# Attention and W_o products in two parts: the high copies' matmuls ahead of the low copies' wait

## What is computed

```python
scores = jnp.einsum('bhqd,bhkd->bhqk', q, k) * scale
scores = jnp.where(causal[None, None], -jnp.inf, scores)
probs = jax.nn.softmax(scores.astype(jnp.float32), axis=-1).astype(q.dtype)
attn = jnp.einsum('bhqk,bhkd->bhqd', probs, v)
...
attn = attn + io
out = attn.transpose(0, 2, 1, 3).reshape(B, S, NH * VD) @ W_o
```

## Time and profile before

| | us |
|---|---|
| median of 3 runs | 686.48 |
| lowest and highest of them | 684.96, 688.63 |
| the profiled execution's own time | 685.76 |
| its span, first to last instruction | 683.9 |

### The profile page before, as it was taken

How to read it: one execution, slowest core, us unless ns; L and a number is a source line. 1 busy time by engine, 2 the same in 40 slices (tenths; PEclk the granted TensorE clock), 3 DMA queues, 4 the chain that set the end, 5 groups by cost and what they waited for, 6 DMA issues and landing times.

```text
span 683.9 us, 14087 instructions
## 1 busy us (share of the span) xinstructions
PE 645.7 (94%) x4456; PEld 582.5 (85%) x4456; DVE 474.8 (69%) x1291; ACT 400.3 (59%) x934; POOL 371.9 (54%) x331
## 2 busy tenths in 40 slices
PE   8899989999999999999999999999999999889895
PEld 5788987898889988898889888988899888779895
DVE  4877367565766667666856586658666667897996
ACT  4884346744764475646664757456744767445552
POOL 7873368463844473456627472738454715431564
PEclk9999999999999999999999999999999999999998
DMA  7307142410451046103610342114510482000001
GB/s 233 115 2 176 41 93 50 114 56 16 109 132 54 0 99 154 54 0 92 146 46 23 92 101 60 54 46 92 115 54 0 108 240 75 10 1 1 1 17 47
DMA packets 23551, 49.85 MB, mean 73 GB/s; under 512 B 3168, under 2 KB 16352, under 8 KB 21600
## 3 DMA queue, kind: packets, MB, share of 16 engines
q1 hardware_dynamic: 22144, 47.82, 27.3%
q10 hardware_dynamic: 1376, 1.64, 0.7%
HBM read 16.94 MB, written 1.05 MB: 26 GB/s over the span
## 4 chain that ended last, share of the span: by engine, by line
PE 55%; DVE 14%; ACT 13%; issue 11%; POOL 4%; DMA 1%; DVEq 0%; ACTq 0%; POOLq 0%; SPq 0%
PE J L840 9%; PE J L842 9%; PE J L841 9%; PE J L873 4%; ACT Pb L1157 4%; DVE PTl L1298 4%; ACT kvraw L1252 3%; PE SC L860 3%; DVE SC L1367 3%; PE SC L862 3%; PE SC L861 3%; PE SC L864 3%; PE SC L863 3%; POOL rstd L711 3%; ACT PTh L1140 2%
## 5 line engine op out<-in xcount | busy, mean ns | idle before, releaser
L1298 DVE TENSOR_TENSOR PTl<-J,PTh 128x512 fp32r<-128x512 f32 (+1 forms) x192 | 102.8, 553 | 67.4 <-ACT PTh L1140 66.4
L1157 ACT ACTIVATE Pb<-SC,nm 128x128 f32<-128x128 f32 (+7 forms) x128 | 94.9, 741 | 54.8 <-DVE nm L1367 54.3
L1367 DVE CUSTOM_DVE_ANT_0 SC<-SC,mask 128x128 f32<-128x128 f32 (+7 forms) x128 | 97.1, 759 | 21.2 <-PE SC L864 20.0
L873 PE MATMUL J<-ident,Pb 128*128 128x128 f32 x576 | 88.9, 280 | 6.4 <-ACT Pb L1157 5.1
L840 PE MATMUL J<-PTh,Vh 128*128 128x256 f32 x320 | 88.7, 277 | 6.4 <-DVE PTl L1298 6.3
L1140 ACT ACTIVATE PTh<-J 128x512 fp32r<-128x512 f32 (+1 forms) x192 | 88.1, 492 | 8.3 <-PE J L873 7.6
L841 PE MATMUL J<-PTl,Vh 128*128 128x256 f32 x320 | 89.5, 280 | 0.0
L842 PE MATMUL J<-PTh,Vl 128*128 128x256 f32 x320 | 89.5, 280 | 0.0
L873 PEld LDWEIGHTS J<-ident,Pb 128*128 128x128 f32 x576 | 64.3, 141 | 15.4 <-ACT Pb L1157 6.8
L840 PEld LDWEIGHTS J<-PTh,Vh 128*128 128x128 f32 x320 | 60.2, 188 | 13.9 <-DVE PTl L1298 12.8
L860 PE MATMUL SC<-KNh,QNh 128*128 128x128 f32 (+2 forms) x192 | 69.3, 361 | 0.1
(11 more groups left out here) (305 smaller groups left out, 1886.5 us busy)
## 6 DMA issues: line engine op xcount, KB each, us to landing
KK<-RK SPq DMA_DIRECT2D x30, 512.0 KB, 6.3
QS<-RQh SPq DMA_DIRECT2D x15, 256.0 KB, 7.5
QS<-RQl SPq DMA_DIRECT2D x15, 256.0 KB, 6.5
KX<-KX SPq DMA_DIRECT2D x14, 256.0 KB, 2.3
QX<-QX SPq DMA_DIRECT2D x14, 256.0 KB, 2.4
r_kv<-in_W_ckv SPq DMA_DIRECT2D x7, 384.0 KB, 3.5
r_o<-in_W_o SPq DMA_DIRECT2D x18, 128.0 KB, 2.1
r_qn<-in_W_qT SPq DMA_DIRECT2D x16, 128.0 KB, 2.1
```

The source lines that it names most:

```text
L873: last = pe.transpose(o[:, tile(j - 4 * c)], Pb[i % 2][:, tile(j)], ident[:, :])
L1157: act.activation(Pb[i % 2][:, w], SC[i % 2][:, s], ACT.Exp, bias=nm[:, i % 2:i % 2 + 1], scale=-1.0, accum_out=sm[:, b, i:i + 1]).then_inc ...
L1298: dve.tensor_tensor(o, i, h.bitcast(F32), ALU.subtract).then_inc(done[kind], 1)
L1367: dve.tensor_tensor_reduce(out=SC[i % 2][:, s], in0=SC[i % 2][:, s], in1=mask[:, 128 * (7 - i):S], scale=-SCALE, scalar=HIGH, op0=ALU.add, ...
```

## The change

In `pv` the three matmuls of each key block are no longer together. First come, for all blocks, the two that read the high copy PTh (with Vh and with Vl); the step waits for the high copies alone, `hi["tc"]`. Then it waits for `pt_lo`, and then come the matmuls with PTl for all blocks. In `wo` the first wait is for `hi["pv"]`; the wait for `done["pv"]` stands before the third matmul, the first to read ATl. The matmuls are the same in number and size, and their order in the sum changes. The other engines' code is as before.

```diff
--- before.py
+++ after.py
@@ -879,10 +879,14 @@
                         pe.wait_ge(done["vs"], g // 2 + 1)
                 elif g == 0:
                     pe.wait_ge(done["vs"], h + 2)
+                parts = [(j, slice(0, 256) if j <= 2 * g else slice(128, 256)) for j in range(2 * g + 2)]
+                pe.wait_ge(hi["tc"], NCH * h + CH0[2 * g + 2])
+                for j, q in parts:
+                    mm(o[:, q], lhsT=Vh[b][:, j, :], rhs=PTh[:, j, q], start=j == 0, stop=False)
+                    mm(o[:, q], lhsT=Vl[b][:, j, :], rhs=PTh[:, j, q], start=False, stop=False)
                 pe.wait_ge(pt_lo, NCH * h + CH0[2 * g + 2])
-                for j in range(2 * g + 2):
-                    q = slice(0, 256) if j <= 2 * g else slice(128, 256)
-                    last = three(o[:, q], Vh[b][:, j, :], Vl[b][:, j, :], PTh[:, j, q], PTl[:, j, q], j == 0, j == 2 * g + 1)
+                for j, q in parts:
+                    last = mm(o[:, q], lhsT=Vh[b][:, j, :], rhs=PTl[:, j, q], start=False, stop=j == 2 * g + 1)
                 return last
 
             def side(c, o):
@@ -1021,10 +1025,14 @@
                 if kind == "pv":
                     last = pv(u, b, c, o)
                 if kind == "wo":
-                    pe.wait_ge(done["pv"], count("pv", u, c))
+                    pe.wait_ge(hi["pv"], count("pv", u, c))
                     for t in range(2):
-                        last = three(o[:, 256 * t:256 * t + 256], ATh[c % 2][:, tile(t)], ATl[c % 2][:, tile(t)],
-                                     ABh[b][:, 256:512], ABl[b][:, 256:512], True, True)
+                        z, ah, al = slice(256 * t, 256 * t + 256), ATh[c % 2][:, tile(t)], ATl[c % 2][:, tile(t)]
+                        mm(o[:, z], lhsT=ah, rhs=ABh[b][:, 256:512], start=True, stop=False)
+                        mm(o[:, z], lhsT=ah, rhs=ABl[b][:, 256:512], start=False, stop=False)
+                        if t == 0:
+                            pe.wait_ge(done["pv"], count("pv", u, c))
+                        last = mm(o[:, z], lhsT=al, rhs=ABh[b][:, 256:512], start=False, stop=True)
                 if kind == "side":
                     if c == 0:
                         pe.wait_ge(ld_side, LD_SIDE)
```

## The result

| | before | changed |
|---|---|---|
| median of 8 runs, us | 686.73 | 682.61 |
| lowest to highest | 684.96 to 688.63 | 681.20 to 684.23 |
| ratio, 95% interval | | 0.9937 (0.9919 to 0.9954) |
| profiled execution: time, span, clock | 685.76, 683.9, 0.992 | 682.62, 680.8, 0.991 |

The kernel is 4.1 us faster; forecast were 681.6 us and 4.9 us less.

What follows compares the result with a forecast made beforehand. TensorE was busy nearly throughout, but the chain that ended last ran only 55% over it. Terms 3.05 + 0.62 + 1.2 = 4.9 us gave a forecast median of 681.6 us, range 679.0 to 684.8.

Steps and rivals of the forecast that it cites:

- group 3 of odd heads, 1 to 11 and 13: Attention product no longer held by the low copy: 6 x 0.51 = 3.05 us in the loop, 0.62 at head 13.
- group 3 of head 0: Attention product then waits, by its bank, for the last low copy but one, ready 0.59 us earlier.
- group 3 of head 14: Same as in head 0: start moves by 0.59 us; the two together give 1.2 us.
- other stalls, order, waits: Attention-product stalls in groups 0, 2 and first and last heads, matmul order and added waits: 0 us.
- W_o products: Low ATl asked for after two matmuls; already there before nearly every one of these steps: gain 0.
- Behind both, ACT and DVE wait for this product: Group 3 of heads 0 and 14: ACT and DVE wait behind it; 2 x 0.59 = 1.2 us in all.
- Added waits: 64 in attention products and 64 in W_o products; taken as 0, between 0 and 11.5 us.
- upper end: W_o product's second matmul 0.21 behind the first, 0.09 over regular: 128 x 0.09 = 11.5 us for the added waits.
- Narrow matmuls: 128-wide matmuls at an attention product's end, two before the low part, one behind: -1.8 to +2.8 us, taken as 0.
- (1): Rival: another ACT, DVE and POOL chain through the pair takes half the gain, 684.1 us; chance 0.20.
- (2): Rival: the half-clock stretch from 569.6, worth 1.7 us, may not come with less idle time, 679.9 us; chance 0.15.
- (3): Rival: added waits cost 0.09 us each at W_o third matmuls and first low attention matmuls, 693.1 us; chance 0.05.

Runs made afterwards that it cites:

- odd_g3: Kernel before with the new order and late wait only in group 3 of the odd heads, 8 of 64 attention products: 683.32 us, ratio 0.9948.
- wo_only: Kernel before with only the W_o products changed, attention products as before: 687.44 us, ratio 1.0001.
- not_odd_g3: Changed kernel with group 3 of the odd heads left as before: 685.84 us, ratio to before 0.9977.
- order_only: Changed kernel with both late waits put back to the start of their products: 686.86 us, ratio to before 0.9997.
- wo1_before: Kernel before with only the odd heads' group 1 W_o product moved behind tile 7's score product, all pairs but the last: 682.98 us, ratio 0.9939.
- met_waits: Changed kernel with 512 more waits, all met, in the attention products: 682.05 us, ratio to before 0.9927.

## Why the prediction was right

The forecast was 681.6, the result 682.61 and 681.83. Its terms, read from the segments above where the clock was alike:

| term | forecast, us | measured, us | from |
|---|---|---|---|
| group 3 of odd heads, 1 to 11 and 13 | 3.67 | 3.55 | odd_g3 against wo_only: 0.38 + 3.12 + 0.05 |
| group 3 of head 0 | 0.59 | 0.56 | not_odd_g3 against wo_only, to head 1 |
| group 3 of head 14 | 0.59 | 0.34 | the same, last column |
| other stalls, order, waits | 0 | 0.4 to 0.5 | not_odd_g3, third column, 0.38 (order_only has 433.69 there, 0.35); 434.04 - 430.47 - 3.12 |
| W_o products | 0 | 0 | wo_only, third column |
| sum | 4.9 | 4.9 | |

That the sums agree to 0.1 us is partly luck: head 14 and the odd heads gave 0.25 and 0.12 less than their terms, and the order, forecast at 0, gave 0.35 more.

**Group 3 of the odd heads** was right in mechanism and size. The price came from start-to-start times, 0.40 for the start and 0.11 for the second matmul; the profile's own column of idle time shows 0.24 of it and would have given half.

**Head 0** was right: in the changed kernel its product still waits for a low copy by DVE, now the last but one, by the bank. DVE and PE of the changed kernel at this place:

```profile
89.62 1.28 DVE L1306 TENSOR_TENSOR PTl<-J,PTh 128x512 fp32r<-128x512 f32 x2
...
90.03 0.28 PE L864 MATMUL SC<-KK,QS 128*128 128x256 f32 x1
...
90.36 0.39 PE L885 MATMUL J<-PTh,Vh 128*128 128x256 f32 x1
```

The first of the two copies ends at 89.62 + 0.69 = 90.31, and the product starts 0.05 behind it. From the last score matmul it is 0.33 us, 1.03 before: the start moved by 0.7, not by 0.59. The 0.56 of the table come from a column in which two executions of one kernel differ by 0.5, so this term is known only roughly. The wait of 0.8 us in the table of waits is the same one of head 14.

**Head 14** was sized too high. "Behind both, ACT and DVE wait for this product" is the step that failed. Its start moved by 0.7 us too (35.77 us behind that of head 13 in wo_only, 35.08 in not_odd_g3), but 4.5 us later DVE is nearly full (busy for 10.68 of 12.00 us from 596 to 608 in the trace of before), and half of the gain ended there. One of its additions lasts longer once it comes earlier. DVE's timeline of wo_only, then of not_odd_g3, at the pair of additions:

```profile
600.73 1.29 DVE L1554 TENSOR_TENSOR acc<-acc,row 128x512 f32<-128x512 f32 x2
```

```profile
599.18 1.62 DVE L1564 TENSOR_TENSOR acc<-acc,row 128x512 f32<-128x512 f32 x2
```

The 0.33 us are just what is given back. It is the first addition of the two that grows, from 0.69 to 1.01 or 1.02 us. GpSimd works on another tensor beside both. In the seven traces with the long addition it starts 0.2 us behind the start of GpSimd's instruction, and in the seven with the regular one 0.7 to 0.9 behind it; why that makes it slower stays open.

**The other stalls** at 0 were right: a pair takes 72.40 us without them and 72.41 with them, in the same order. But they were so for a reason that holds only as long as their cover: in wo1_before the cover of group 2 is gone, and the change is worth 0.31 us a pair more.

**Added waits** at 0 were right. The upper end of 0.09 us a wait, read from a W_o product's second matmul, was no wait's price. PE's timeline of the changed kernel, a W_o product with no idle time before it:

```profile
271.89 0.36 PE L1031 MATMUL J<-ABh,ATh 128*128 128x256 f32 x1
272.09 0.28 PE L1032 MATMUL J<-ABl,ATh 128*128 128x256 f32 x1
272.21 0.28 PE L1035 MATMUL J<-ABh,ATl 128*128 128x256 f32 x1
```

The second matmul, without a wait, is still late, 0.20 behind the first, but the third, in front of which the added wait stands, follows the second by 0.12; over the 64 products this spacing is 0.118 (median), with the wait and without it. **Narrow matmuls** at 0: order_only shows 0.05 us a pair less, 0.35 in its third column, clear of the loop's scatter and well inside the -1.8 to +2.8 that the prediction allowed.

**The rivals.** (1) needed half of the gain to go into other waits; only head 14's did. (2) had the granted clock at 569.6 fall because of the stall at 558.25. It does not: in wo_only and order_only that stall is kept, and the last segment runs without a half-clock stretch (124.64 us, order_only 124.65), while the changed kernel without the stall had one at 600 to 606. The price of the stretch at 569.6 was too high as well: 1.7 us forecast, 1.0 measured. By "TensorE: Matmul & The Clock Gate", Part 1, of the Trainium skill less idleness can only help this clock; no trace here bears that out for this stall. (3) is excluded at both of its places, by wo_only for the W_o products and by the spacing of 0.171 us in order_only and in the changed kernel for the first low matmul; met_waits shows the same where work is queued.

The first measurement's 4.1 us is less than the sum's 4.9. Its interval (0.9919 to 0.9954, 3.2 to 5.6 us) holds the sum, and the changed kernel's profiled execution, whose time is its median, lost 3.3 us to half-clock stretches where that of before lost 1.0.

## What to carry to other kernels

Where an engine waits for two copies of a product and the second is made from the first, put the work that needs only the first in front; the wait behind it costs nothing where work is queued. Count on what one wait costs from start-to-start times and follow the chain from it: here 8 of 64 products gave 70% of the gain, and the table of waits, which lost 4.7 us in one row and won 4.2 in others, told neither which nor how much. A stall that is free because something else is late has to be priced again when that something is mended, and the larger gain may lie there: an accumulation in front of a row maximum was worth more than the change itself.

## What was not expected of the hardware

- 512 more waits, all met and nearly all carried by weight loads, in a stream of matmuls with 0.12 us between starts changed the time by nothing that can be measured, under 0.001 us each.
- After two 128-wide matmuls, 0.06 and 0.11 us apart, a 256-wide one is followed 0.17 us later instead of 0.12, with or without a wait. The weight loads keep their 0.11 us there, and a group 3 took 2.65 us in either order.
- The first of two additions on DVE took 1.02 us instead of 0.69 where it started 0.2 us behind an instruction of GpSimd. Moving the product that led to it 0.7 us earlier brought half of that.
- Stretches at half the TensorE clock come at different places in executions of one kernel, and the three priced here cost 1.0 to 1.7 us each. Two single traces of this kernel differ by as much as half of the change's whole effect for that alone, so segments had to be compared with such stretches on both sides or on neither.
